# A transformer layer with gated sparse feed-forward on one core: convolution outputs kept in rows, their sums on GpSimd, their transposes in phase two, and three edits of queue order

## What is computed

```python
q, k, v = relu(ln(x) @ Wq + bq), ...            # then causal softmax(q k^T / sqrt(512)) v
x = x + ln(relu(attention @ Wo + bo))
h = ln(x)                                       # rows n, 512 = 128 channels of 4
xc = einsum('ngf,gf->ng', h.reshape(n, 128, 4), conv_w) + conv_b   # once "out", once "in"
mean, var = xc over all n rows                  # batch norm: needs all 8192 rows
xa = gelu((xc - mean) * rsqrt(var + 1e-5) * gamma + beta)
score = softmax(xa @ lin_w.T + lin_b)           # 512 wide; keep the 32 largest of each row
y = (h @ weight) * top32(score_out) + (h * top32(score_in)) @ weight + bias
x = x + ln(y)
```

## Time and profile before

| | us |
|---|---|
| median of 3 runs | 2106.03 (2103.82 to 2106.3) |
| the profiled execution, its own time | 2106.83 |
| its span in the profile | 2105.0 |

### The profile page before, as it was taken

One profiled execution on the slowest core, in us unless ns is written; L12 is line 12 of the kernel. 1 busy time (PEld: TensorE's weight loads), 2 busy tenths in 40 slices (PEclk: granted clock), 3 DMA queues, 4 the chain that ended last, 5 costly groups with the idle time before them and its releaser, 6 DMA issues. The chain is left out here.

```text
span 2105.0 us, 30881 instructions
## 1 busy us (share of the span) xinstructions
PE 2003.7 (95%) x9340; PEld 933.3 (44%) x9340; DVE 1525.5 (72%) x3459; ACT 1144.1 (54%) x2396; POOL 925.4 (44%) x1118
## 2 busy tenths in 40 slices
PE   8999999999999999999999999967999999999997
PEld 4444444444444444444444444422444444444443
DVE  6666554676645567655557665567999999999998
ACT  5454333354434354443335433324888888888885
POOL 2222212132121232312123211122899999999998
PEclk9999999999999999999999999987999999999998
DMA  5334333444242524434334342451122222222322
GB/s 182 86 85 104 76 94 71 110 113 107 70 106 64 102 80 112 102 80 101 73 98 110 84 91 57 117 148 39 61 86 96 93 94 96 86 85 92 105 76 70
DMA packets 301594, 194.86 MB, mean 93 GB/s; under 512 B 223858, under 2 KB 241394, under 8 KB 301428
## 3 DMA queue, kind: packets, MB, share of 16 engines
q1 hardware_dynamic: 301428, 192.88, 34.7%
HBM read 82.69 MB, written 58.72 MB: 67 GB/s over the span
## 5 line engine op out<-in xcount | busy, mean ns | idle before, releaser
L579 PE MATMUL psum<-hT,w_hi 128*128 128x512 f16 (+1 forms) x1544 | 458.0, 378 | 0.4 <-DVE w_lo L1012 0.4
L579 PE MATMUL psum<-v,pT 128*128 128x512 f16 x1632 | 362.7, 379 | 5.4 <-DMA pT<-phl 5.2
L579 PE MATMUL psum<-kT,qT 128*128 128x512 f16 (+3 forms) x1920 | 363.4, 347 | 0.0
L579 PE MATMUL psum<-hT,w_lo 128*128 128x512 f16 (+1 forms) x772 | 292.1, 378 | 0.0
L579 PEld LDWEIGHTS psum<-kT,qT 128*128 128x128 f16 x1920 | 181.2, 98 | 175.1
L779 ACT ACTIVATE raw<-psum,bqkv_s 128x512 f32<-128x512 f32 x192 | 131.4, 684 | 223.8 <-PE psum L579 221.5
L1269 DVE MAX8 c<-cut 128x8 f32<-128x512 f32 x384 | 248.1, 697 | 0.0
L579 PEld LDWEIGHTS psum<-v,pT 128*128 128x128 f16 x1632 | 159.3, 98 | 195.4 <-issue 7.2
L1391 POOL TENSOR_SCALAR ve<-mv 128x1 f32<-128x1 f32 x64 | 20.7, 324 | 507.3 <-DVE mv L1089 506.7
L790 ACT ACTIVATE sS<-sS,nm 128x128 f32<-128x128 f32 (+7 forms) x64 | 76.9, 1201 | 287.0 <-DVE nm L1063 287.0
L579 PEld LDWEIGHTS psum<-hT,w_hi 128*128 128x128 f16 x1544 | 151.3, 98 | 173.3 <-DVE w_lo L1012 0.7
(11 more groups left out here) (138 smaller groups left out, 3729.4 us busy)
## 6 DMA issues: line engine op xcount, KB each, us to landing
xg<-x SPq DMA_DIRECT2D x64, 256.0 KB, 5.0
xr<-x SPq DMA_DIRECT2D x64, 256.0 KB, 2.9
x_scratch<-xr SPq DMA_DIRECT2D x64, 256.0 KB, 2.3
h_scratch<-hb SPq DMA_DIRECT2D x64, 256.0 KB, 3.0
h<-h_scratch SPq DMA_DIRECT2D x64, 256.0 KB, 2.8
x<-x_scratch SPq DMA_DIRECT2D x64, 256.0 KB, 3.0
out<-zn SPq DMA_DIRECT2D x59, 256.0 KB, 2.0
xc_scratch<-xcT SPq DMA_DIRECT2D x64, 128.0 KB, 2.2
```

The source lines that it names most:

```text
L579: mm = nc.tensor.matmul(outp, stat(a), mov(c), start=(n == 0 and k == 0), stop=(n == total - 1 and k == 2))
```

## The change

- `convolution` writes its sums in rows to dsq (`[P, 2, 2, 2*P]`: two tiles, values and squares). The x item is gone but for tile 0, where PE multiplies with a matrix of 1/128 and ACT copies the result, a mean row, to pilot. For tiles 0 to 59 POOL, at lag 4, subtracts pilot, squares, and adds both to csum; for tiles 60 to 63 DVE subtracts and squares as part of the convolution. SP stores the deviations at lag 6, so one half is added to the loop.
- After the P products PE transposes the first group's deviations and sums csum and the last four tiles over rows with single-column matmuls into bank 5. DVE's two bn_aggr become four small steps, POOL's five small ones become two beside them and four after.
- In phase two PE transposes four tiles' deviations (eight matmuls) into banks 6 and 7 before the logits of every fourth tile, and gelu reads them from there. F and I keep one bank each.
- Queue order, in the first group after each batch's first (`opening`, g = 1, 5, 9, 13): SP's hT transposes of tile 1 move from h 4 to h 5, behind the P transposes of the fourth tile; PE takes one vo stage before that tile's P product. At the end SP's first loads of phase two move from half PREP + 4 to PREP + 5, behind the P transposes of the last tile.

```diff
+def opening(g):
+    return 0 < g <= NG and GROUP * (g - 1) % TILES == 0
...
     items = stages(H) + attention if H % HALF < 2 else attention + stages(H)
-    if due(H, 4) is not None:
-        items.append(("x", due(H, 4)))
+    if opening(H // HALF) and H % HALF == 6:
+        items = stages(H)[:1] + attention + stages(H)[1:]
+    if due(H, 4) == 0:
+        items.append(("x", 0))
...
-        F_BANK = [psum[:, n, :] for n in (4, 5)]
-        I_BANK = [psum[:, n, :] for n in (6, 7)]
+        F_BANK, I_BANK = psum[:, 4, :], psum[:, 5, :]
+        X_BANKS = psum[:, 6:8, :].rearrange("p b (t r n) -> p (b t) r n", t=2, r=2)
...
                 def store_xc(T):
-                    sp.wait_ge(x_ev.sem, x_ev.at(T))
-                    sp.dma_start(xc_d[T], xcT[:, T % 2].rearrange("p r n -> p (r n)")).then_inc(xc_out[T % 2].sem, 16)
+                    signal, i = deviation_of(T)
+                    sp.wait_ge(signal.sem, signal.at(i))
+                    sp.dma_start(xc_d[T], dsq[:, T % 2, 0, :]).then_inc(xc_out[T % 2].sem, 16)
...
-                    for lag, move in ((-1, load_residual), (2, store_x1), (4, store_h2), (5, store_xc)):
+                    for lag, move in ((-1, load_residual), (2, store_x1), (4, store_h2), (6, store_xc)):
...
                     if h == 5 and pv_tile(H) is not None:
                         transpose_p(GROUP * (g - 1) + 3)
+                    if h == 5 and opening(g):
+                        transpose_h(g + 1, 1)
                     rows_of(H)
...
                     if h == 4 and g + 1 < NG:
                         transpose_h(g + 1, 0)
-                        transpose_h(g + 1, 1)
+                        if not opening(g):
+                            transpose_h(g + 1, 1)
...
-                    if H == PREP + 4:
+                    if H == PREP + 5:
                         for k in range(2):
                             load_conv(k)
...
+                def conv_columns(k):
+                    pe.wait_ge(xc_in[k % 2].sem, xc_in[k % 2].at(k // 2))
+                    need(pe, gelu_ok, -1 if k < 1 else gelu_at(GROUP * (k - 1) + 3))
+                    for j in range(GROUP):
+                        for s in range(2):
+                            mm = nc.tensor.matmul(X_BANKS[:, j, s, :], xcg[:, k % 2, j, s, :], idn[:], is_transpose=True,
+                                                  start=(j % 2 == 0 and s == 0), stop=(j % 2 == 1 and s == 1), skip_group_check=True)
+                    mm.then_inc(ct_ps.sem, 1)
+                def channel_sums():
...
+                    for T in range(OWN, TS):
+                        for m, ready in ((0, dev_last), (1, sq_last)):
+                            pe.wait_ge(ready.sem, ready.at(T - OWN))
+                            for s in range(2):
+                                mm = add(dsq[:, T % 2], m, s, False, T == TS - 1 and m + s == 2)
+                        mm.then_inc(sums_ps.sem, 1)
...
+                pe.wait_ge(o_ev.sem, o_ev.at(TS - 1))
+                conv_columns(0)
+                channel_sums()
...
                 for i in range(LAST):
+                    if i % GROUP == 0 and i // GROUP + 1 < TS // GROUP:
+                        conv_columns(i // GROUP + 1)
...
-                        need(pe, tf_ok, m - 2)
-                        expand(F_BANK[m % 2], h2T[:, m % 2], full_ps)
+                        need(pe, tf_ok, m - 1)
+                        expand(F_BANK, h2T[:, m % 2], full_ps)
...
-                        need(pe, tin_ok, k - 2)
-                        expand(I_BANK[k % 2], xsT[:, k % 2], in_ps)
+                        need(pe, tin_ok, k - 1)
+                        expand(I_BANK, xsT[:, k % 2], in_ps)
...
-                        i = nc.scalar.activation(xa[:, slot, j0:j1, s, :], xcg[:, slot, j0:j1, s, :], ACT.Gelu, bias=bn_bi[:, s:s + 1],
+                        i = nc.scalar.activation(xa[:, slot, j0:j1, s, :], X_BANKS[:, j0:j1, s, :], ACT.Gelu, bias=bn_bi[:, s:s + 1],
...
-                        need(dve, x_ps, T - 2)
-                        nc.vector.tensor_reduce(xcs[:, T % 2, P * r:P * (r + 1)], prod[:].rearrange("p (g f) -> p g f", f=4),
+                        need(dve, xc_out[T % 2], T // 2 - 1)
+                        if T < OWN + 2:
+                            need(dve, csum_ok, T - 2)
+                        else:
+                            dve.wait_ge(sums_ps.sem, sums_ps.at(T - 2 - OWN))
+                        nc.vector.tensor_reduce(dsq[:, T % 2, 0, P * r:P * (r + 1)], prod[:].rearrange("p (g f) -> p g f", f=4),
                                                 AX.X, ALU.add).then_inc(xc_ok.sem, 1)
+                    if T >= OWN:
+                        deviations(T)
-
-                def conv_stats(T):
...
+                def deviations(T):
+                    dve.wait_ge(xc_ok.sem, xc_ok.at(2 * T + 1))
+                    nc.vector.tensor_tensor(dsq[:, T % 2, 0, :], dsq[:, T % 2, 0, :], pilot[:], ALU.subtract).then_inc(dev_last.sem, 1)
+                    dve.wait_ge(dev_last.sem, dev_last.at(T - OWN))
+                    nc.vector.tensor_tensor(dsq[:, T % 2, 1, :], dsq[:, T % 2, 0, :], dsq[:, T % 2, 0, :], ALU.mult) \
+                        .then_inc(sq_last.sem, 1)
...
-                for s in range(2):
-                    i = nc.vector.bn_aggr(bn_mv[:, s, :], bn_all[:, :, s, :])
-                i.then_inc(bn_stat, 1)
+                        lambda: nc.vector.tensor_scalar(bn_dev[:], S_BANK[:, 0:2], 1.0, None, ALU.mult),
+                        lambda: nc.vector.tensor_tensor(bn_sq[:], bn_dev[:], bn_dev[:], ALU.mult),
+                        lambda: nc.vector.tensor_tensor(bn_var[:], S_BANK[:, 2:4], bn_sq[:], ALU.subtract),
+                        lambda: nc.vector.tensor_scalar(bn_ve[:], bn_var[:], 0.0, EPS, ALU.max, ALU.add))):
...
+                def channel_sum(T):
+                    pool.wait_ge(x_ev.sem, x_ev.at(0))
+                    wait_apart(pool, xc_ok, xc_ok.at(2 * T + 1))
+                    nc.gpsimd.tensor_tensor(dsq[:, T % 2, 0, :], dsq[:, T % 2, 0, :], pilot[:], ALU.subtract).then_inc(dev_ok.sem, 1)
...
+                    nc.gpsimd.tensor_tensor(dsq[:, T % 2, 1, :], dsq[:, T % 2, 0, :], dsq[:, T % 2, 0, :], ALU.mult) \
+                        .then_inc(dsq_ok.sem, 1)
...
+                    nc.gpsimd.tensor_tensor(csum[:], csum[:], dsq[:, T % 2], ALU.add).then_inc(csum_ok.sem, 1)
...
                     if due(H, 1) is not None:
                         residual(due(H, 1))
+                    if due(H, 4) is not None and due(H, 4) < OWN:
+                        channel_sum(due(H, 4))
```

More of the change, by code:

```diff
@@ L321, in layer_block, with deviation_of @@
         x_ev = sig("x_ev")
-        bn_ok = sig("bn_ok")
+        dev_ok = sig("dev_ok")
+        dsq_ok = sig("dsq_ok")
+        csum_ok = sig("csum_ok")
+        sums_ps, bn_off = sig("sums_ps"), sem("bn_off")
+        dev_last, sq_last = sig("dev_last"), sig("sq_last")
+        OWN = TS - GROUP
+        def deviation_of(T):
+            return (dev_ok, T) if T < OWN else (dev_last, T - OWN)
         def m_bank(item):
@@ L474, in load_conv @@
                 def load_conv(k):
-                    need(sp, gelu_ok, -1 if k < 2 else gelu_at(GROUP * (k - 2) + 3))
+                    need(sp, ct_ps, k - 2)
                     for n in range(2):
@@ L639, in product, with pilot_mean @@
                     mm.then_inc(pv_ps.sem, 1)
-                def conv_transposes(T):
+                def pilot_mean(T):
                     bank = take_m(("x", T))
                     pe.wait_ge(xc_ok.sem, xc_ok.at(2 * T + 1))
-                    for r in range(2):
-                        mm = nc.tensor.transpose(bank[:, P * r:P * (r + 1)], xcs[:, T % 2, P * r:P * (r + 1)], idn[:])
-                    mm.then_inc(x_ps.sem, 1)
+                    pe.wait_ge(setup_pool, 3)
+                    nc.tensor.matmul(bank[:, 0:2 * P], avg[:], dsq[:, T % 2, 0, :], start=True, stop=True).then_inc(x_ps.sem, 1)
                 def transposed(src, bank, signal):
@@ L669, in _, with add @@
                         else:
-                            conv_transposes(*at)
+                            pilot_mean(*at)
+                def conv_columns(k):
[7 more added lines that the diff above has]
+                def channel_sums():
+                    def add(src, m, s, first, last):
+                        return nc.tensor.matmul(S_BANK[:, 2 * m + s:2 * m + s + 1], src[:, m, P * s:P * (s + 1)], rowmean[:],
+                                                start=first, stop=last, skip_group_check=True)
+                    pe.wait_ge(vo_lo.sem, vo_lo.at(TS - 1))
+                    pe.wait_ge(s_ev.sem, s_ev.at(chunk_at(TS, 0) - 1))
+                    pe.wait_ge(csum_ok.sem, csum_ok.at(OWN - 1))
+                    for m in range(2):
+                        for s in range(2):
+                            add(csum, m, s, m + s == 0, False)
+                    for T in range(OWN, TS):
```

(35 more changed lines are left out.)

63 lines of the change are left out of this document (37 added, 26 removed).

## The result

The changed kernel takes 2090.03 us (median of 4 runs, 2088.72 to 2090.68), the one before 2105.33 beside it: ratio 0.9924, 95% interval 0.9911 to 0.9938. The profiled execution took 2089.64 us with a span of 2087.8, 17.2 us less than before; the forecast for it was 18.2 less.

What follows compares the result with a forecast made beforehand. PE was taken to bound phase one, DVE phase two, with a chain of waiting steps between. Terms -12.8 - 5.2 - 0.5 + 0.3 = -18.2 us gave 2087.8 us on the median; range 2083 to 2096.

Steps and rivals of the forecast that it cites:

- Transposes leave phase one: Phase one, PE: sixty pairs of x-item matmuls go, 0.216 us each, less about 0.2 for tile 0: -12.8 us.
- P transposes: Phase one, fourth tiles: queue edits remove all three PE waits for P transposes: -5.2 us, bounds 0 and -5.2.
- POOL's sums: Phase one: POOL's deviation, square and sum of tiles 0 to 59, 2.7 us a tile, are hidden: cost 0.
- rival 1: Phase one: POOL's extra 164 us hold DVE, P comes later, PE's 5.2 us of waits stay: 2093.0 us; chance 0.12.
- Shorter ring: Phase one: DVE's reduce may wait for SP's store of T-2, 3.4 us at tile 58: 0, bounds 0 and +3.4.
- The turn: Between the phases: bn_aggr replaced, -3.6, against DVE's added deviations and a store wait: -0.5 us, bounds -3.6 and +2.
- Phase two: Transposes before every fourth tile's logits: steady state costs 0, first tiles may add POOL lag: +0.3 us, bounds 0 and +11.
- rival 2: Phase two turns to POOL's pace, 0.88 us every four tiles: +11, 2099 us; in part +3, 2091; chance 0.11.
- rival 3: Phase one: DVE stops at the shorter ring, 30 reduces waiting for stores; at 0.8 us each 2112 us; chance 0.04.
- rival 4: The turn: added DVE work hides and PE's clock stays above 0.55: -22 to -24, 2083 us; chance 0.07.
- rival 5: Phase one: an equally slow feeder of PE fills the gap the pairs leave; time within 0.2%; chance 0.04.

Runs made afterwards that it cites:

- the last run: Changed kernel plus low halves of k first, all queues reordered, columns one tile earlier, 38 unread matmuls, ACT's normalisation of tile 62 before relu of 63: 2084.82 us.

## Why the prediction was right, and where not

The time came out as forecast, 2090.03 us against 2087.8, but in part by luck. Phase one and the turn gained 3.7 us less than forecast (15.4 for 18.0, and 0.6 lost for 0.5 gained). In the two profiled executions the part from the first gelu on gave 2.7 us more than forecast, a difference that executions of one kernel show among themselves. So the profiled gain, 17.2 us, lies 1.0 from the forecast of 18.2; the medians' gain, 15.3 us, lies 2.9 from it.

- **Transposes leave phase one, -12.8: right.** From the run with the queue edits alone to the one with POOL's squares and sums cut, both without a wait worth naming, the last P product moves from 1395.27 to 1382.44: 12.8 us. POOL's deviations are in the second run, so their cost, if any, is in this number.
- **P transposes, -5.2: right by themselves, 5.6 us.** Taken with POOL's sums they are worth twice that (11.4 us in the medians), because they are a reserve and POOL uses it up.
- **POOL's sums, cost 0: the step that failed.** They cost 3.0 us at the last P product, 0.4 more or less by what executions differ. The work itself was priced well, 2.9 us a tile (859, 662 and 1353 ns) for 2.7; that it is hidden was wrong. The text had the 734 ns beside 689 and weighed them against DVE's idle share of 40%; that share is a mean, and the P chain is not. It was the mechanism of rival 1, at 60% of its price (3.0 of 5.2): it brought back one of the waits for P, and made k late at two score tiles. The three sizes are steps from one run to the next, so they add up to the measured end (-12.8 - 5.6 + 3.0 = -15.4) by themselves; with the edits taken as the last step they are worth 13.3 us at this end (1398.8 without them), and the other two together only 2.1.
- **Shorter ring, 0: right.** DVE waits for the store at four reduces, 5.8 us in all, longest 3.1 at tile 58 (forecast 3.4), and PE does not feel it: in the run with POOL's sums cut, DVE waits 3.4 and 4.5 us at tiles 58 and 59, and PE has no wait at all.
- **The turn, -0.5: +0.6, inside its bounds.** bn_aggr went as priced. Two deviations of 0.42 us cost 0.92 us a tile, priced 0.95. From the last reduce to the gelu it is 4.9 us, not 4.2: the last eight sums take 1.87 us, priced 0.7, and 1.06 us where the extra matmuls held the clock at 0.97. The run with the deviations on POOL shows that giving this work away is worse.
- **Phase two, +0.3: no difference clear of what executions differ by.** From the first match_replace to the end it took 2.3 us less in this pair. But with the phase two of before, two profiled executions took 670.2 us (before) and 668.8 (queue edits alone), and with the changed one, seven (its own and six runs, the extra matmuls not counted) took 667.7 to 670.1. Most of the spread is one place, DVE's tile 3: before lost 1.7 us in it, with PE's granted clock at 0.92 there; four of the seven lost 1.0 to 1.4 us and three up to 0.2. So neither a gain nor the forecast's small cost is shown. No transposes are felt at the logits: in the changed kernel's profile DVE has no wait for them after the first match_replace. New are 0.2 us at each of eight later tiles.

Rivals 2, 3, 4 and 5 didn't come. Of rival 2 its first half is there: the transposes reach POOL in PE's backlog of the first tiles, and POOL's lag reaches DVE from tile 31, for 1.5 us in all (before, once, 0.3 us at tile 51).

## What to carry to other kernels

Work given to an idle engine is paid where it holds the engine whose chain feeds the bound; look for it in what stands beside it in the timeline, not in shares of busy time. An edit that gives reserve and one that uses it have to be priced together: 5.8 us alone were 11.4 in company. In a stretch where every engine waits for another, moving one engine's work moved the wait (+1.7 and +0.6 us in two runs); reordering all queues gained 2.2 us, less than hoped. And the profiles of one execution each differ by 2 us in phase two alone: a term of that size needs several of them.

## What the runs showed of the hardware that I had not expected

A wait of PE costs more than its length where the clock falls: after 3.76 us without a matmul the granted clock was 0.50 and twelve matmuls took 4.44 instead of 2.75 us; after 2.29 us it was 0.50 too, and 48 took 12.12 instead of 10.52. After waits of 2.40, 3.19 and 3.32 us it stayed at 1.00, so the length of a wait alone does not tell. At the turn the loss can be bought back with work that nothing reads: 48 extra matmuls saved 3.1 us in the profile and some 2 in the median (2088.07 against 2090.03, whose intervals overlap). In the last run ten of them, at a clock of 0.50, stood in the way of the sums.

Which DVE operations are held beside POOL's goes by kind: a low half (two inputs) took 1.22 us instead of 0.69 and four normalisations 3.15 instead of 1.91, while statistics and reduces kept their 0.7 us throughout.
